# Scan in pairs of octets, with the products that read z as quarters of the TensorE array, and the values' weight loaded in the mixing layer

## The reference, cut to what matters

```python
def _ssm(x, A, B_ssm, C_ssm, D_ssm):          # x: [batch, length, 512 channels], 16 states per channel
    Abar = jax.nn.sigmoid(A)
    def step(h, xt):
        h = h * Abar + xt[..., None] * B_ssm
        y = jnp.einsum('bcs,cs->bc', h, C_ssm) + D_ssm * xt
        return (h, y)
    ...
x1 = x @ w1_w.T + w1_b
x_conv = _silu(_depthwise_conv(x1, conv_w))
x_ssm = _ssm(x_conv, A, B_ssm, C_ssm, D_ssm)
v = _silu(x @ v1_w.T + v1_b)
return x_ssm * v @ w2_w.T + w2_b
```

## Time and profile before

| what | us |
|---|---|
| median of three runs | 2051.77 |
| the profiled execution, its own time | 2050.9 |
| its span | 2049.1 |
| TensorE busy in the span | 2034.8 |
| VectorE busy | 1435.1 |
| ScalarE busy | 1094.5 |
| POOL busy | 772.5 |
| idle time of VectorE before L785, for TensorE | 56.5 |

### The profile page before, as it was taken

How to read it: one execution, slowest core, us unless ns; L and a number is a source line. 1 busy time by engine, 2 the same in 40 slices (tenths; PEclk the granted TensorE clock), 3 DMA queues, 4 the chain that set the end, 5 groups by cost and what they waited for, 6 DMA issues and landing times.

```text
span 2049.1 us, 27189 instructions
## 1 busy us (share of the span) xinstructions
PE 2034.8 (99%) x8987; PEld 1615.0 (79%) x8987; DVE 1435.1 (70%) x2869; ACT 1094.5 (53%) x1843; POOL 772.5 (38%) x778
## 2 busy tenths in 40 slices
PE   9999999999999999999999999999999999999998
PEld 6887888544588888888888888888888888888887
DVE  6998875656666666666666775677767767777776
ACT  4555555323355555555555556655555555555553
POOL 1001111344434444443444443244444444444444
PEclk9999999999999999999999999999999999999999
DMA  5766663887544443443544443322222222222211
GB/s 200 258 212 220 197 217 126 274 266 220 187 133 142 133 143 121 137 138 120 160 125 130 144 129 123 134 73 73 73 93 87 78 90 86 72 72 72 73 42 42
DMA packets 215476, 277.35 MB, mean 135 GB/s; under 512 B 47784, under 2 KB 146344, under 8 KB 212776
## 3 DMA queue, kind: packets, MB, share of 16 engines
q1 hardware_dynamic: 202072, 251.83, 38.0%
q10 hardware_dynamic: 13264, 23.79, 3.3%
HBM read 169.53 MB, written 101.83 MB: 132 GB/s over the span
## 4 chain that ended last, share of the span: by engine, by line
PE 93%; DVE 2%; DMA 2%; ACT 2%; issue 1%; POOL 1%; SPq 0%; ACTq 0%; POOLq 0%; DVEq 0%
PE bank L105 24%; PE bank L106 24%; PE bank L107 24%; PE bank L1562 8%; PE bank L2106 3%; PE bank L914 3%; PE bank L939 3%; PE bank L936 3%; PE bank L1524 1%; DMA bv_row<-in_L_attn_bv 0%; DMA b_w_raw<-in_L_attn_w_w 0%; PE bank L1578 0%; DVE e_w_lo L1933 0%; DMA d_v<-scr_v 0%; DMA d_qx<-d_qb 0%
## 5 line engine op out<-in xcount | busy, mean ns | idle before, releaser
L105 PE MATMUL bank<-e_ring,e_w_hi 128*128 128x512 f32 x512 | 200.7, 392 | 0.0
L106 PE MATMUL bank<-e_ring,e_w_hi 128*128 128x512 f32 x512 | 199.3, 389 | 0.0
L107 PE MATMUL bank<-e_ring,e_w_lo 128*128 128x512 f32 x512 | 199.2, 389 | 0.0
L1562 PE MATMUL bank<-d_kh,d_nat 128*128 128x512 f32 x768 | 192.0, 399 | 0.0
L1826 POOL TENSOR_TENSOR e_x<-e_x,e_beta 128x512 f32<-128x512 f32 x64 | 91.4, 1448 | 217.7 <-ACT e_y L1869 217.7
L1880 ACT ACTIVATE e_kr<-bank 128x512 f32<-128x512 f32 x64 | 38.0, 594 | 243.7 <-PE bank L107 243.7
L1562 PEld LDWEIGHTS bank<-d_kh,d_nat 128*128 128x128 f32 x768 | 139.7, 188 | 27.7
L1951 DVE TENSOR_TENSOR e_ring<-e_mixed,e_ring 128x512 fp32r<-128x512 f32 x128 | 93.5, 731 | 88.0 <-ACT e_ring L1844 88.0
L1808 POOL TENSOR_TENSOR e_x<-e_x,e_ff 128x512 f32<-128x512 f32 x64 | 83.3, 1302 | 175.4 <-DVE e_ff L2017 175.4
L1439 DVE TENSOR_TENSOR d_nat<-d_xn,d_nat 128x512 fp32r<-128x512 f32 x64 | 63.8, 997 | 102.1 <-ACT d_nat L1297 102.1
L1183 POOL TENSOR_TENSOR d_kacc<-d_kacc,d_kr 128x512 f32<-128x512 f32 x64 | 82.7, 1292 | 137.9 <-ACT d_kr L1270 137.9
(11 more groups left out here) (215 smaller groups left out, 6109.7 us busy)
## 6 DMA issues: line engine op xcount, KB each, us to landing
scr_v<-b_vt SPq DMA_DIRECT2D x64, 256.0 KB, 2.7
scr_z<-b_zt SPq DMA_DIRECT2D x64, 256.0 KB, 2.1
c_z<-scr_z SPq DMA_DIRECT2D x64, 256.0 KB, 4.5
scr_y<-c_y ACTq DMA_DIRECT2D x64, 256.0 KB, 4.0
d_x<-in_L_attn_x SPq DMA_DIRECT2D x64, 256.0 KB, 5.4
d_v<-scr_v SPq DMA_DIRECT2D x32, 512.0 KB, 5.8
scr_x<-d_x SPq DMA_DIRECT2D x64, 256.0 KB, 2.8
...
```

The costliest lines, as they stand in the source:

```text
L105: eng.matmul(out, lhs[hi], rhs[hi], start=first, stop=False, skip_group_check=onto)
L106: eng.matmul(out, lhs[hi], rhs[lo], start=False, stop=False, skip_group_check=onto)
L107: return eng.matmul(out, lhs[lo], rhs[hi], start=False, stop=last, skip_group_check=onto)
L1562: mm = pe.matmul(BG[c][:, :], s[:, i, cols], r[:, j, :], start=M % NTB == 0 and i == j, stop=M % NTB == NTB - 1 and i == 1, skip_group_che ...
```

## The change

Octets are scanned in pairs, p = 0 to 31. A block of `into` or `toep` joins only rows and columns of one channel. The change uses this: the 128 rows of z of an octet are taken as two halves (i = 0, 1, four channels each), and each table is built as 128 rows by 64 columns instead of 128 by 128. Where before one product of 128 x 128 was made per octet and table, now four quarters of 64 x 64 are made per pair and table (`quarters`): half i of octet k of the pair goes into bank i, rows k x 64 to k x 64 + 63. So a bank then holds one half of the channels of both octets, and `outof`, the decay rates and the y addresses follow that arrangement (`by_state`, `y_of`, the addresses of scr_kern).

Further: `own(p)` waits for z and tables of both octets. `within(p)` starts both Y banks at once and waits until both outputs of the pair before are taken. `out_of(t)` is the product that was at L939. VectorE's scans of a pair wait for all four quarters. Two pairs of state-input banks stand in SB (banks 6, 7, 0, 1), and FB, where the weight is turned, shrinks to two banks, so `turn_weight` runs at octets 24, 26, 28 and 30 and from its third piece on waits for VectorE. Tables are built six octets ahead, `into` and `toep` as 64 columns instead of 128. The z loads of a pair are released together. The four loads of `wv` are issued at steps 10 to 13 of the mixing layer, and TensorE's wait for them moves into `values`. The store of `kern` is cut into four.

The diff, without what only sizes or rearranges host arrays and the turned weight's bank numbers on VectorE:

```diff
@@ -301,9 +301,14 @@
             store_v(g)
             if g == 8:
                 sp.wait_ge(k_step, 3)
-                sp.dma_start(scr["kern"].rearrange("o c x -> c o x"), kpad[:, :, :]).then_inc(kern_out, 16)
+                k = scr["kern"]
+                for h in range(2):
+                    for i in range(2):
+                        to = bass.AP(k.tensor, (h * OCTET + i * OCTET // 2) * 2 * CHUNK,
+                                     [[2 * CHUNK, OCTET // 2], [2 * OCTET * 2 * CHUNK, NO // 2], [1, 2 * CHUNK]])
+                        sp.dma_start(to, kpad[h * OCTET // 2:(h + 1) * OCTET // 2, i:NO:2, :]).then_inc(kern_out, 16)
             if g == 9:
-                sp.wait_ge(kern_out, 16)
+                sp.wait_ge(kern_out, 4 * 16)
                 k = scr["kern"]
                 for c in range(OCTET):
                     one = bass.AP(k.tensor, c * 2 * CHUNK, [[1, CHUNK], [OCTET * 2 * CHUNK, NO], [1, CHUNK]])
@@ -666,7 +671,9 @@
 
 def phase_scan(nc, sh, ins, scr, keep, banks, areas, late, mix):
     KT, D, NO, NCB, NCH, NS, B = sh.KT, sh.D, sh.NO, sh.NCB, sh.NCH, sh.NS, sh.B
-    Z, Y, TABS = 6, 4, 3
+    Z, Y, TABS = 6, 4, 6
+    HALF = P // 2
+    EIGHTHS = OCTET // 2
     turned_x, first_weight, tokens = [areas[n] for n in ("turned_x", "first_weight", "tokens")]
     project = keep["project"]
 
...
@@ -701,12 +708,13 @@
     HI = 2 * KT
     q_step, f_turned, f_hi = sem("c_q_step"), sem("c_f_turned"), sem("c_f_hi")
 
-    FB, YB, SB = banks[0:4], banks[4:6], banks[6:8]
+    FB, YB, SB = banks[2:4], banks[4:6], (banks[6:8], banks[0:2])
     into_t, toep_t, out_pow, mask8 = keep["into_t"], keep["toep_t"], keep["out_pow"], keep["mask8"]
     ident = keep["ident"]
     z_of = scr["z"].rearrange("(o c) r n -> o (c r) n", c=OCTET)
-    y_of = scr["y"].rearrange("(o c) m n -> o (c m) n", c=OCTET)
-    TURN_AT, WEIGHTS_AT, QUANTISE_AT = 24, 32, 7
+    y_of = scr["y"].rearrange("(p k i e) m n -> p i k (e m) n", k=2, i=2, e=EIGHTHS)
+    mask4 = keep["mask4"]
+    TURN_AT, WEIGHTS_AT, QUANTISE_AT = {24: 0, 26: 1, 28: 2, 30: 3}, 32, 7
     QUANTISE_STEPS = [(k, part) for k in range(5) for part in ((0, 1), (None,))[k in (1, 2)]]
     QUANTISED_AT, WEIGHT_PIECES_AT, BIASES_AT = 1, 6, 30
     MIX_IN_AT, MIX_PREPARE_AT, MIX_BANKS_AT, MIX_HEAD_AT = 38, 40, 42, 61
@@ -740,7 +748,7 @@
             if o == NO // KT:
                 for h in range(2):
                     sp.wait_ge(*project["z"][h])
-            sp.wait_ge(y_full, o - Z + 1)
+            sp.wait_ge(y_full, (o - Z) // 2 * 2 + 1)
             load_z(o)
             if 30 <= o < 30 + mix["tiles_ahead"]:
                 mix["load_x"](o - 30)
@@ -758,14 +766,17 @@
         pool.wait_ge(*project["powers"])
         pool.wait_ge(keep["tables_in"], 64 + 16 * OCTET)
         blocks = mask8.unsqueeze(2).broadcast_to([P, OCTET, CHUNK])
+        half_blocks = mask4.unsqueeze(2).broadcast_to([P, EIGHTHS, CHUNK])
         for o in range(NO):
             i = o % TABS
             if o >= TABS:
                 pool.wait_ge(y_full, o - TABS + 1)
-            for tile, rows in ((into[i], into_t[:, o, :]), (toep[i], toep_t[:, o, :]),
-                               (outof[i], out_pow[:, o, 1:CHUNK + 1])):
-                nc.gpsimd.tensor_tensor(tile[:, :, :], rows.unsqueeze(1).broadcast_to([P, OCTET, CHUNK]), blocks,
+            for tile, rows in ((into[i], into_t[:, o, :]), (toep[i], toep_t[:, o, :])):
+                nc.gpsimd.tensor_tensor(tile[:, :, :], rows.unsqueeze(1).broadcast_to([P, EIGHTHS, CHUNK]), half_blocks,
                                         ALU.mult).then_inc(tab_done, 1)
+            nc.gpsimd.tensor_tensor(outof[i][:, :, :],
+                                    out_pow[:, o, 1:CHUNK + 1].unsqueeze(1).broadcast_to([P, OCTET, CHUNK]), blocks,
+                                    ALU.mult).then_inc(tab_done, 1)
             if o == TABS:
                 nc.gpsimd.memset(keep["kv"][:, :, :, :], 0.0).then_inc(keep["set"], 1)
             if o == 28:
@@ -777,12 +788,12 @@
 
     def vector(dve):
         def scan(o):
-            dve.wait_ge(own_full, o + 1)
+            dve.wait_ge(own_full, 4 * (o // 2 + 1))
             if o >= 2:
                 dve.wait_ge(y_full, o - 1)
             rate = keep["decay"][:, o:o + 1].broadcast_to([P, NCB - 1])
             for b in range(B):
-                nc.vector.tensor_tensor_scan(state[o % 2][:, b, 1:], rate, SB[o % 2][:, b * NCB:(b + 1) * NCB - 1],
+                nc.vector.tensor_tensor_scan(state[o % 2][:, b, 1:], rate, SB[o // 2 % 2][o % 2][:, b * NCB:(b + 1) * NCB - 1],
                                              0.0, ALU.mult, ALU.add).then_inc(state_done, 1)
 
         def weight_low(i, kt, tile, raw):
...
@@ -855,15 +866,14 @@
 
         def store(o):
             act.wait_ge(y_done, o + 1)
-            act.dma_start(y_of[o], yo[o % Y][:, :]).then_inc(y_stored[o % Y], 16)
+            act.dma_start(y_of[o // 2, o % 2], yo[o % Y][:, :]).then_inc(y_stored[o % Y], 16)
 
         def weight_high(i, kt, tile, raw):
             if kt == 0:
                 act.wait_ge(raw_in[i], 16 * KT)
             nc.scalar.activation(tile[:, 0, kt, :], raw[:, kt, :], ACT.Copy).then_inc(w_hi, 1)
 
-        pieces = [(w2_raw, "L0_attn_w2_w", raw_in[0]), (wk_raw, "L1_attn_Wk", raw_in[1]),
-                  (wv, "L1_attn_Wv", late["wv_in"])]
+        pieces = [(w2_raw, "L0_attn_w2_w", raw_in[0]), (wk_raw, "L1_attn_Wk", raw_in[1])]
         for o in range(NO):
             take(o)
             if QUANTISED_AT <= o < QUANTISED_AT + KT:
@@ -875,16 +885,16 @@
                     act.wait_ge(*project["z"][h])
                     act.wait_ge(*project["v"][h])
                 act.wait_ge(*project["powers"])
-            if WEIGHT_PIECES_AT <= o < WEIGHT_PIECES_AT + 2 * 3 * KT and (o - WEIGHT_PIECES_AT) % 2 == 0:
+            if WEIGHT_PIECES_AT <= o < WEIGHT_PIECES_AT + 2 * 2 * KT and (o - WEIGHT_PIECES_AT) % 2 == 0:
                 i, kt = divmod((o - WEIGHT_PIECES_AT) // 2, KT)
                 tile, name, done = pieces[i]
                 act.dma_start(tile[:, kt, :], ins[name][:, kt, :]).then_inc(done, 16)
             if o in (BIASES_AT, BIASES_AT + 2, BIASES_AT + 4):
                 mix["load_bias"]((o - BIASES_AT) // 2)
-            if TURN_AT <= o - 1 < TURN_AT + KT:
-                kt = o - 1 - TURN_AT
+            if o - 1 in TURN_AT:
+                kt = TURN_AT[o - 1]
                 act.wait_ge(f_turned, kt + 1)
-                nc.scalar.activation(wf[:, 0, kt, :], FB[kt][:, :], ACT.Copy).then_inc(f_hi, 1)
+                nc.scalar.activation(wf[:, 0, kt, :], FB[kt % 2][:, :], ACT.Copy).then_inc(f_hi, 1)
             if WEIGHTS_AT <= o < WEIGHTS_AT + 2 * KT:
                 i, kt = divmod(o - WEIGHTS_AT, KT)
                 weight_high(i, kt, *((w2, w2_raw), (wk, wk_raw))[i])
@@ -906,13 +916,33 @@
                 mix["set_sums"](o - NO + 3)
 
     def tensor(pe):
-        def own(o):
-            pe.wait_ge(z_in[o % Z], 16 * (o // Z + 1))
-            pe.wait_ge(tab_done, 3 * (o + 1))
-            if o >= 2:
-                pe.wait_ge(state_done, B * (o - 1))
-            pe.matmul(SB[o % 2][:, :], into[o % TABS][:, :, :].rearrange("p c s -> p (c s)"), zo[o % Z][:, :],
-                      start=True, stop=True).then_inc(own_full, 1)
+        def quarters(bank, tables, p, stop):
+            for i, k in ((0, 0), (1, 1), (0, 1), (1, 0)):
+                o, rows = 2 * p + k, slice(i * HALF, (i + 1) * HALF)
+                yield pe.matmul(bank[i][k * HALF:(k + 1) * HALF, :],
+                                tables[o % TABS][rows, :, :].rearrange("p e s -> p (e s)"), zo[o % Z][rows, :],
+                                start=True, stop=stop, skip_group_check=not stop)
+
+        def own(p):
+            for o in (2 * p, 2 * p + 1):
+                pe.wait_ge(z_in[o % Z], 16 * (o // Z + 1))
+            pe.wait_ge(tab_done, 3 * (2 * p + 2))
+            if p >= 2:
+                pe.wait_ge(state_done, B * (2 * p - 2))
+            for mm in quarters(SB[p % 2], into, p, True):
+                mm.then_inc(own_full, 1)
+
+        def within(p):
+            if p:
+                pe.wait_ge(y_done, 2 * p)
+            for mm in quarters(YB, toep, p, False):
+                pass
+
+        def out_of(t):
+            pe.wait_ge(state_done, B * (t + 1))
+            pe.matmul(YB[t % 2][:, :], outof[t % TABS][:, :, :].rearrange("p c m -> p (c m)"),
+                      state[t % 2][:, :, :].rearrange("p b n -> p (b n)"), start=False, stop=True,
+                      skip_group_check=True).then_inc(y_full, 1)
 
         def pairs_of(ot, kt):
             first = ot * D + kt // 2 * 2 * P + kt % 2
@@ -921,27 +951,25 @@
         def turn_weight(kt):
             if kt == 0:
                 pe.wait_ge(q_step, len(QUANTISE_STEPS))
+            if kt >= 2:
+                pe.wait_ge(w_lo, KT + kt - 1)
             for ot in range(KT):
```

(30 more changed lines are left out.)

27 lines of the change are left out of this document (14 added, 13 removed).

## The result

| | before | after |
|---|---|---|
| median of the runs, us | 2052.43 (2051.49 to 2053.37, 4 runs) | 2280.36 (2276.88 to 2282.16, 4 runs) |
| profiled execution, us | 2050.9 | 2282.16 |
| its span, us | 2049.1 | 2280.3 |

The changed kernel takes 1.1109 times as long, interval 1.1089 to 1.1128. I had forecast 2032 us, and my range ended at 2080. (The forecast started from 2051.77 us, the median of the first three of the four runs of before.) In the profiled executions the difference of the spans is 231.2 us.

What follows compares the result with a forecast made beforehand. TensorE, busy 99%, was taken to bound the kernel; 31 pairs x (5.15 - 4.45) = 21.7 us less, + 0.5 + 1.5, gave 19.7 less: span 2029.4, forecast 2032 us, range 2012 to 2080 (its own 2020 to 2042).

Steps and rivals of the forecast that it cites:

- other covers: Scan work beside TensorE and z loads (takes, VectorE's scans, POOL's tables, kernel table's store, turned weight): all stays hidden.
- Quarters: Scan products `own` and `within`: four quarters side by side cost what one product costs, 0.86 us.
- rival 1: Quarters in the scan overlap only with a neighbour: eight take 3.86 us, a pair 5.91, total 2076 us; chance 0.38.
- (a): Bound chosen for the scan's quarters: four side by side cost one product, 2 x 0.429 = 0.86 us.
- The changes of shape: TensorE switching between quarters and full products, twice per pair: up to 0.16 us each, taken as 0.33 us.
- my sum for TensorE alone: TensorE's time for a pair of octets without waits: 0.86 + 0.86 + 1.72 + 0.33 = 3.77 us.
- z's ring: Six z buffers, only three pairs, make z loads late next: a pair takes 4.2 to 4.7 us, taken as 4.45.
- 2P = L + 2.91: Where z loads decide: P a pair's time, L release to later landing (5.5 to 6.5 us), 2.91 us products and shape changes.
- rival 3: The z buffers keep up in the scan: a pair takes 3.77 us, 44 us less, total 2008; chance 0.08.
- The take: ScalarE's take before `within`: 0.80 us, hidden by `own`, 0.86; each 0.1 us more exposes 3 us over 32 pairs.
- Wv: Four 256 KB loads moved from scan to mixing layer, 2.5% of scan transfers; first reader runs long after, cost 0.
- The ends: Scan start +0.5 us; mixing layer's first weights still in time, 3.1 us early before; 1.5 us given back for SyncE's issues.

Runs made afterwards that it cites:

- The third experiment: The kernel before with only its y store changed to the new pattern (2 blocks of 64 rows): 2276.89 us, 1.1096 times before.
- The eight-tile kernel: The pair-store kernel with eight z tiles instead of six, so z loads are released one pair earlier: 2033.50 us, 0.9908 times before.
- the pair-store kernel: The changed kernel with a pair's y stores issued behind its second take as two 256 KB transfers, one per half of 64 rows: 2045.78 us, 0.9968.
- the kernels with four and with eight blocks: The kernel before with only its y store's pattern changed, to four blocks of 32 rows (2115.58 us) or eight of 16 rows (2058.57 us).
- the kernel with the other order of quarters: The eight-tile kernel with neighbouring quarters on the same rows, where before they alternated: 2031.93 us, 0.9899 times before.

## Why the prediction was wrong, point by point

**The step that failed: the store of y.** I went through "other covers" and put a price on POOL, on VectorE, on the kernel table's store ("nothing") and on the takes. The y store has the same bytes, the same queue and the same number of issues, and its new `y_of` never got a price: it stood in the sum at nothing, without a reason. Its issue went from 0.33 to 4.3 us, and the two engines that carry it became the scan's bound. The third experiment shows that this one line of addresses is the whole loss: alone in the kernel before it costs 225 us, where the changed kernel lost 228. I had asked that the take be hidden by `own` with 0.06 us to spare, and that each 0.1 us more would cost 3 us; this was the place to ask what else stands on ScalarE's queue. The rule cited above from the Trainium skill (DMA: Bandwidth & Descriptors) would have put the store on two engines; the prediction did not use it.

**Quarters: right.** The forecast took four quarters at the price of one product, and rival 1 had 0.38. The eight-tile kernel shows it at full clock, where nothing waits:

```profile
413.34 1.09 PE L929 MATMUL bank<-c_z,c_into 64*64 64x512 f32 x8
414.25 1.04 PE L929 MATMUL bank<-c_z,c_toep 64*64 64x512 f32 x8
415.22 1.98 PE L950 MATMUL bank<-c_state,c_outof 128*128 128x512 f32 x4
417.13 1.09 PE L929 MATMUL bank<-c_z,c_into 64*64 64x512 f32 x8
```

Eight passes are done in 1.09 us, and the next group starts 0.91 us after them; one after the other they would need 8 x 0.429 = 3.43. The windows of 0.1 us over the quarters alone (PE busy and records, PEld busy and records, clock, DMA share, GB/s) show two waves:

```profile
413.30:413.40 0.10, 0.06 (x4) 0.06 (x5) 1.00 0.85 307
...
413.70:413.80 0.10, 0.10 (x4) 0.00 (x0) 1.00 0.67 246
413.80:413.90 0.10, 0.10 (x8) 0.00 (x0) 1.00 0.97 328
```

Four passes run from 413.34, and the second four join them at 413.8. Rival 1 wanted the quarters one step of 0.43 us apart and 3.86 us for eight of them; two groups took 0.91 + 0.97. Its mechanism is refuted. The statement of the Trainium skill behind it (TensorE: Matmul & The Clock Gate, The mechanism), that matmuls start in the order of the program, did not lead to quarters one step apart here. What the Trainium skill has in TensorE: Matmul & The Clock Gate, Measured speedup vs the span model, spoke for (a), and the trace agrees: 3.43 against 0.91 us is 3.8 times.

**The changes of shape: right, within 0.03 us.** The starts above lie 0.91, 0.97 and 1.91 us apart, and the passes alone would need 0.86, 0.86 and 1.72: 0.05 + 0.11 + 0.19 = 0.35 us a pair. The 0.05 stands between two groups of the same shape, so the two changes cost 0.30 where I had 0.33, and the 16 loads, which I had put at nothing, can be at most what is left. The pair repeats after 3.79 us; my sum for TensorE alone was 3.77.

**z's ring: the right mechanism, at the edge of its range; the loads beside it: too small.** With the store mended, the scan of the pair-store kernel runs from 371.4 to 529.5 us, 158 us for 32 pairs. That is 4.94 us a pair on average, but the average mixes two things. Without the first pair and the one late pair shown above, `own` repeats after 4.72 us, where I took 4.45 from 4.2 to 4.7. By 2P = L + 2.91, L was 6.5 us, the end of my 5.5 to 6.5. I had put in the spread of one landing; each pair waits for the later of two, and this trace has 2.7 to 10.3 us with the same median of 4.7. The late pair is the other term: for SyncE's other issues at the end of the scan I gave back 1.5 us, with the time of the transposes as the only figure and nothing for the bytes, and that pair took 11.6 - 4.7 = 6.9 us more than the others. A rough count: 29 x 0.27 = 7.8 for the pairs, 5.4 for the late one, 1.6 for the start, together 14.8, and this profiled span misses the forecast one by 2044.0 - 2029.4 = 14.6.

After its longest waits TensorE's clock is lower as well. In this window of that kernel, which holds the wait of 7.7 us, the mean granted clock is 0.90, and right behind that wait eight passes take 1.98 us instead of 1.09:

```profile
470.00:520.00 50.00, 38.32 (x186) 11.55 (x182) 29.27 (x55) 13.81 (x23) 20.73 (x57) 0.90 0.80 242
```

That left 6.5 us of the 19.7 that were forecast. With eight z tiles the scan takes 143 us, 24 less than before. It is not the 32 x (5.15 - 3.79) = 44 us of rival 3: its three products still have 6.5 + 4.9 + 5.3 = 16.7 us of idle time before them.

**The take: thin, as said, and the late store showed itself there.** I wrote that I would be wrong if the waits named it, and they do, 170.6 us. I had priced the take as 0.80 us behind its product and nothing ahead of it on ScalarE.

**Wv: as forecast.** The loads are issued at 875 to 910 us of the changed kernel, their first reader runs at 1184 us, and the trace names no wait for them.

**The ends.** The start was to come 0.5 us later. It comes 4.5 us later in the changed kernel and 1.2 to 5 us later in its variants. But the kernels with four and with eight blocks, whose opening phase is that of before, also begin 2.1 and 1.9 us later; like the changed one they show a wait of some 2 us for `b_first` in the opening phase, which is 0.4 us in the profile of before, 1.7 in the kernel with the other order of quarters and missing in its twin with eight tiles. So some 2 us come and go without the change; the rest was not tested. The end was to stay covered by 3.1 us; with stores on two engines it was not, 17.0 us.

That the best version (2032 to 2033.5 us) meets the number of the forecast is chance: it has no store on two engines, and a ring that the forecast did not have.
